# Expert feed-forward after attention: high part and remainder of w1 kept in w1's own column order, weight loads with a column step of four

## The reference, cut to what matters

```python
def _L0_ffn_ref(x, gate_w, w1, w2):        # x: 8 x 512 x 128; w1: 16 x 128 x 512; w2: 16 x 512 x 128
    tokens = x.reshape(-1, D_MODEL)
    capacity = _capacity(s, N_EXPERTS)     # 320 slots for each of the 16 experts
    gate_logits = tokens.astype(jnp.float32) @ gate_w.T
    combine_weights, sec_mask = _top1_router(gate_logits, capacity)
    dispatch = jnp.einsum('sec,sd->ecd', sec_mask.astype(tokens.dtype), tokens)
    h = jax.nn.gelu(jnp.einsum('ecd,edf->ecf', dispatch, w1))
    expert_out = jnp.einsum('ecf,efd->ecd', h, w2)
    out = jnp.einsum('sec,ecd->sd', combine_weights.astype(tokens.dtype), expert_out)
    return out.reshape(x.shape)
...
x = x + ga * _L0_attn_ref(h, ...)          # h = layernorm(x) * (1 + ca) + sa
x = x + gb * _L0_ffn_ref(h, ...)           # h = layernorm(x) * (1 + cb) + sb
```

## Time and profile before

| | |
|---|---|
| median of 3 executions | 231.9 us (229.3 to 232.04) |
| profiled execution, its own time | 229.94 us |
| span of the profiled execution | 227.7 us |
| mean granted TensorE clock | 0.951 of full speed |
| TensorE matmul busy | 196.4 us (86%) |
| TensorE weight load busy | 157.9 us (69%) |
| VectorE busy | 151.1 us (66%) |
| ScalarE busy | 145.5 us (64%) |
| GpSimd busy | 117.3 us (52%) |

### The profile page before, as it was taken

The page is one execution under the profiler, slowest core; times in us unless marked ns, Lnnn a source line. Parts: engine busy times, 40 slices in busy tenths (PEclk is TensorE's granted clock), DMA queues, the critical chain, the costliest instruction groups (busy, mean ns, idle before and its releaser), DMA issues.

```text
span 227.7 us, 4034 instructions
## 1 busy us (share of the span) xinstructions
PE 196.4 (86%) x1177; PEld 157.9 (69%) x1177; DVE 151.1 (66%) x472; ACT 145.5 (64%) x425; POOL 117.3 (52%) x143
## 2 busy tenths in 40 slices
PE   7995999999999999859867487999999999999151
PEld 4885587797888787647653234887887888889141
DVE  2669679999989989968863408074765856662121
ACT  4396679999999789857544721686586685824000
POOL 6317443131888284748557460000785577577733
PEclk9999799999998899999999679999999999999957
DMA  5999999239340051142343216999969724410100
GB/s 154 290 350 360 359 331 354 77 88 286 95 169 16 3 188 46 38 150 101 113 159 119 83 36 136 366 358 358 341 203 308 250 78 143 138 40 27 35 23 13
DMA packets 37284, 38.60 MB, mean 170 GB/s; under 512 B 2591, under 2 KB 31334, under 8 KB 37264
## 3 DMA queue, kind: packets, MB, share of 16 engines
q1 hardware_dynamic: 33936, 31.29, 43.4%
q0 software_dynamic: 3328, 7.07, 8.7%
HBM read 19.19 MB, written 18.95 MB: 167 GB/s over the span
## 4 chain that ended last, share of the span: by engine, by line
PE 56%; DVE 18%; issue 7%; another core or an unknown queue 7%; POOL 5%; ACT 3%; DMA 2%; POOLq 1%; DVEq 0%; SPq 0%; ACTq 0%
PE bank L1280 13%; PE bank L1266 12%; PE bank L1039 4%; PE bank L1057 3%; PE bank L1050 3%; PE bank L1029 2%; PE bank L1083 2%; PE bank L1190 2%; PE bank L1078 2%; PE bank L1109 2%; POOL xh L294 2%; DVE kvsum L780 2%; DVE w1l L955 2%; PE bank L1244 2%
## 5 line engine op out<-in xcount | busy, mean ns | idle before, releaser
L529 POOL DMA_INDIRECT out_dram<-x_all,rest x40 | 44.1, 1101 | 45.5 <-issue 41.4
L503 POOL DMA_INDIRECT dispatched_rows<-rows,slot x32 | 32.2, 1006 | 18.9 <-issue 9.3
L709 ACT ACTIVATE HT<-bank 128x320 f32<-128x320 f32 x64 | 28.0, 438 | 18.2 <-remote 9.1
L1280 PE MATMUL bank<-HT,w 128*128 128x320 f32 x112 | 32.4, 432 | 0.0
L1280 PEld LDWEIGHTS bank<-HT,w 128*128 128x128 f32 x112 | 20.6, 189 | 6.7
L1266 PE MATMUL bank<-xth,w1h 128*128 128x320 f32 x64 | 22.6, 353 | 0.3 <-DVE xtl L961 0.3
L977 DVE SCALAR_TENSOR_TENSOR junk<-bank,rest 128x128 f32<-128x128 f32 x40 | 11.5, 344 | 14.6 <-remote 10.3
L955 DVE TENSOR_TENSOR w1l<-w,w1h 128x1024 fp32r<-128x1024 f32 x8 | 16.1, 2026 | 6.9 <-DMA dispatched_rows<-rows,slot 6.9
L1266 PE MATMUL bank<-xth,w1l 128*128 128x320 f32 x64 | 19.8, 309 | 0.0
L1266 PE MATMUL bank<-xtl,w1h 128*128 128x320 f32 x64 | 19.8, 309 | 0.0
L1004 DVE COPY OT<-bank 128x320 f32<-128x320 f32 x14 | 6.9, 492 | 18.4 <-PE bank L1280 17.4
(11 more groups left out here) (172 smaller groups left out, 503.3 us busy)
## 6 DMA issues: line engine op xcount, KB each, us to landing
w<-in_L_ffn_w_dram SPq DMA_DIRECT2D x16, 512.0 KB, 9.7
dispatched_rows<-blank SPq DMA_DIRECT2D x8, 965.0 KB, 12.2
rest<-dispatched_rows SPq DMA_DIRECT2D x8, 645.0 KB
hin<-dispatched_rows SPq DMA_DIRECT2D x7, 320.0 KB, 10.9
x_all<-in_L_attn_x_dram SPq DMA_DIRECT2D x8, 256.0 KB, 6.1
rows<-gb_row SPq DMA_DIRECT2D x8, 256.0 KB, 3.7
out_dram<-rows SPq DMA_DIRECT2D x8, 256.0 KB
out_dram<-x_all,rest POOLq DMA_INDIRECT x40
```

What stands on the lines that cost most here:

```text
L503: pool.indirect_dma_start(out=disp_d, out_offset=bass.IndirectOffsetOnAxis(ap=slot[:, b, j:j + 1], axis=0), in_=rows[:, b, j, :], in_offse ...
L529: pool.indirect_dma_start(out=out_d.rearrange("b t d -> (b t) d"), out_offset=bass.IndirectOffsetOnAxis(ap=rest[i % RING][:, n, C_TOK - D: ...
L709: act.activation(HT[e][:, f, :], ps_h[c % HB][:, 0:CAP], ACT.Gelu_apprx_tanh).then_inc(h_done, 1)
L1280: last = pe.matmul(ps_o[e], w2[i % RING][:, e, f, :], HT[e][:, f, :], start=(f == 0), stop=(f == NF - 1))
```

## The change

The buffers `w1h` and `w1l` lose the split of their last axis into (4, 128) and keep the 512 columns in the order of `w1`. ScalarE's copy and VectorE's subtraction now read and write densely. The reordering moves to TensorE: the stationary operand of each inner matmul is now every fourth column of `w1h` or `w1l`, 128 elements 16 bytes apart. The number of instructions, their order, the semaphores and the DMAs stay as they are.

```diff
-        w1h, w1l = [[sb(f"{name}{n}", [P, 2, NF, P], f32r) for n in range(2)]
+        w1h, w1l = [[sb(f"{name}{n}", [P, 2, FF], f32r) for n in range(2)]
                     for name in ("w1h", "w1l")]
...
-                act.copy(w1h[i % 2][:, :, :, :], w1[i % RING][:, :, :].rearrange("p e (m f) -> p e f m", f=NF)
-                         ).then_inc(w1h_done, 1)
+                act.copy(w1h[i % 2][:, :, :], w1[i % RING][:, :, :]).then_inc(w1h_done, 1)
...
-                dve.tensor_tensor(w1l[i % 2][:, :, :, :],
-                                  w1[i % RING][:, :, :].rearrange("p e (m f) -> p e f m", f=NF),
-                                  w1h[i % 2][:, :, :, :].bitcast(f32), ALU.subtract).then_inc(w1l_done, 1)
+                dve.tensor_tensor(w1l[i % 2][:, :, :], w1[i % RING][:, :, :],
+                                  w1h[i % 2][:, :, :].bitcast(f32), ALU.subtract).then_inc(w1l_done, 1)
...
-                        last = pe.matmul(ps_h[c % HB][:, 0:CAP], w[i % 2][:, e, f, :],
+                        last = pe.matmul(ps_h[c % HB][:, 0:CAP],
+                                         w[i % 2][:, e, :].rearrange("p (m f) -> p f m", f=NF)[:, f, :],
                                          x[i % 2][:, e * CAP:(e + 1) * CAP], start=(n == 0), stop=(n == 2))
```

## The result

The changed kernel takes 242.17 us (median of four, 239.39 to 242.24) against 231.97 us for the kernel before (four runs, 229.3 to 233.71): a ratio of 1.050, 95% interval 1.044 to 1.057. It is slower, as forecast, by 10 us where 15 were forecast. The profiled execution has a span of 240.5 us and a time of its own of 242.21 us.

What follows compares the result with a forecast made beforehand. TensorE, busy without a break in the experts, was taken as the bound: 229.94 us plus 17.2 us for stepped loads over eight pairs, less 0.05 us at the start, gave 247.1 us, with a range of 229 to 256 us.

Steps and rivals of the forecast that it cites:

- The bound: Stage of the experts: TensorE works without a break, 8.9 us a pair, and hides the other engines' work.
- The splits: Copy to w1h and subtraction to w1l: dense, they save 1.03 and 0.81 us, gaining only 0.05 us before the first pair.
- The load: TensorE's stepped load of 128 columns for inner matmuls: 237 ns against 147 hidden, adding 2.15 us a pair.
- three readers of the memory: ScalarE, VectorE and TensorE's moving operand: 1.84, 1.87 and 1.84 ns per new 16 bytes, giving a load of 237 ns.
- the twelve: A pair's run of 12 inner matmuls behind an outer product: 1.76 us before, 2.8 us forecast.
- the sum: Whole kernel: eight pairs add 17.2 us, the start gives back 0.05 us, 229.94 us becomes 247.1 us.
- The ratios of whole instructions: Alternative load estimates: 111 ns scaled by stepped over dense times of VectorE or ScalarE, 184 or 223 ns.
- First rival: Stepped weight loads stay hidden under the 147 ns matmuls: no change, 229 to 232 us; chance 0.25.
- the 36 ns of room: Inner matmuls: a dense load of 111 ns can grow this much before it exceeds the 147 ns that hide it.
- Second rival: Inner matmuls: load and moving operand reads add up, to 384 ns each, or the clock falls: 256 to 275 us; chance 0.11.
- Third rival: End: waits of 5.37 and 8.17 us hang on GpSimd's backlog; longer experts give back up to 8 us; faster, chance 0.03.

Runs made afterwards that it cites:

- second profile of the kernel before: The kernel before, unchanged, profiled again beside the changed kernel on one chip: ratio 0.999; the kernel before takes 220.38 us there, the changed kernel 232.24.

## Why the prediction was right, and where it was off

**The bound.** It stood: TensorE had no room in a pair, busy in 8.90 of 8.90 us, and the other engines had, VectorE busy in 5.86 us and ScalarE in 5.97. The splits got cheaper by 1.00 and 0.80 us (forecast 1.03 and 0.81), and none of it reached the time of the changed kernel, in the pairs or ahead of the first. What I had not seen is that a shorter subtraction also holds up GpSimd's sends for less: on one chip the 40 sends take 4.2 us more than at 0.97 us each in the kernel before and 3.8 in the changed one. With the changed kernel's long pairs there is no backlog that this could shorten.

**The load.** This term made the sign. The forecast was 237 ns, from three readers of the memory; the measured load is 234 ns (147 + 0.96 / 11). Two of the readers carry it. The third, 147 ns for the 80 pieces of the moving float32r columns, is one point that no run varies, and the 320 plain float32 columns of the outer product, also 80 pieces, follow at 269 ns, so its 1.84 ns can be luck. The forecast of 2.8 us for the twelve (2.75 by the terms of the sum, which leave the first load covered) and 11.05 for the pair met 2.72 and 10.99; the whole stage grew by 16.5 us where 17.2 were forecast. The ratios of whole instructions, which gave 184 and 223 ns, were the worse estimate, because they contain the fixed part and the dense speed of the other engine.

**First rival (hidden).** It fell: 234 ns against 147. The number of columns alone doesn't set the price, since the same 128 columns take 175, 234 and 243 ns at steps of three, four and eight elements of 4 bytes; the count of the 16-byte pieces, 96, 128 and 128, fits them. Only at a step of two did the load stay hidden, with the twelve at 1.76 us. That a load is hidden as long as it is shorter than the distance to the next matmul I had read off alone, and the runs bear it out. At a step of three one load of 175 ns fits both places: 28 ns more behind matmuls that follow at 147 ns (the twelve at 2.07 us) and 66 ns more behind a transpose of 109 (the nine at 1.60). And a load of 234 ns behind an outer product of 269 ns adds nothing (the twelve at 2.37 us with only the high part stepped). The 111 ns of the dense load, and so the 36 ns of room, stay an estimate: matmuls of 16 columns and transposes of 128 follow at the same 110 ns, which points to the load, but no run varies it.

**Second rival (reads add up, or clock).** It fell: the pair's twelve inner matmuls take 2.72 us, not over 3.4, and the clock is 1.00 in the stage.

**Third rival (the end closes up).** This is the step that was mis-sized. I took the end as unchanged in the sum and kept its shortening for the range. It shortened by 6.3 us between the first two profiles and by 4.2 us between the two on one chip. From the forecast of 247.1 us, 0.7 less for the loads, 6.3 less for the end and 2.6 more ahead of the experts make 242.7 us, and the profiled execution took 242.2. The mechanism was right in that GpSimd's backlog goes when pairs get longer, which the kernel with dense loads and long pairs showed by itself. I was wrong on the row: the waits of 5.37 and 8.17 us are not that backlog. In the second profile of the kernel before they are absent and the backlog is there. About 4 us of the first profile's end, 20.65 - 16.7, go with these waits and stay without a cause. Such waits stand in five of the six profiles of two groups of runs, four of them of kernels with short pairs, and in none of the eight of the two others. The first two groups are those in which the kernel before takes 230 to 232 us instead of 220. What releases the waits stays open.

## What to carry to other kernels

Where one engine has no idle time and others have, a permutation belongs in the copy that the others make anyway, even if it doubles their price: here it cost ScalarE 2.04 us instead of 1.04 and VectorE 2.03 instead of 1.23, hidden in the pairs, and on TensorE it added 2.08 us to a pair. A stepped float32 operand was best priced by the number of 16-byte pieces that it touches (1.82 to 1.90 ns for each), at the rate of the engines of the same trace that read with a step (1.84 and 1.87 ns). And when the bound engine gets slower, the queue behind it (here GpSimd's sends) can give back part of it (here 4.2 us of 16.5), so the end has to be costed on its own.

## What the hardware showed

TensorE's weight load of 128 float32r columns takes 175 ns at a step of 12 bytes, 234 at 16 and 243 at 32, and is hidden at 8 under the 147 ns of a matmul (the twelve at 1.76 us). Divided by the 96, 128 and 128 pieces of 16 bytes that is 1.82, 1.83 and 1.90 ns for each, next to ScalarE's 1.84 and VectorE's 1.87. The moving operand shows no sign of being held up meanwhile: a kernel with one stepped load in three pays for exactly that one (0.35 us for four of twelve, 87 ns each), and a stepped load behind a matmul of 269 ns costs nothing (0.61 us for eight stepped loads, seven at 87 ns). A send of GpSimd that starts while VectorE subtracts one SBUF operand from another, 0.97 us by itself, ends some 0.80 us after the subtraction does (0.79 to 0.80 in the second profile of the kernel before, 0.84 to 0.85 in that of the changed one). I had not expected the kernel before to have medians from 219.6 to 232.0 us between groups of runs on different chips.
